# Routed expert layers: joined sums spread over loop turns, row counts placed later, three scatter buffers

## The reference

```python
logits = einsum('bsh,he->bse', x, rw) + rb
vals, idx = top_k(softmax(logits), 2);  vals = vals / vals.sum(-1)
xhat = (x - mean(x)) * rsqrt(var(x) + EPS)
xe = xhat[None] * g + b                                   # per expert
h = gelu(einsum('ebsh,ehf->ebsf', xe, w1) + b1)
y = einsum('ebsf,efh->ebsh', h, w2) + b2
x = einsum('bsh,ebsh->bsh', comb, x[None] + y)            # comb: the two weights, else 0
```

## Time and profile before

| | us |
|---|---|
| median of 3 runs (1640.12 to 1645.81) | 1641.62 |
| the profiled execution | 1646.7 |
| its span | 1644.9 |
| TensorE busy, share of the span | 1418.8, 86% |
| VectorE busy | 1274.0, 77% |
| ScalarE busy | 1120.4, 68% |
| POOL busy | 847.8, 52% |
| mean granted TensorE clock | 0.932 |

### The profile page before, as it was taken

How to read it: one execution, slowest core, us unless ns; L and a number is a source line. 1 busy time by engine, 2 the same in 40 slices (tenths; PEclk the granted TensorE clock), 3 DMA queues, 4 the chain that set the end, 5 groups by cost and what they waited for, 6 DMA issues and landing times.

```text
span 1644.9 us, 36942 instructions
## 1 busy us (share of the span) xinstructions
PE 1418.8 (86%) x11037; PEld 1110.8 (68%) x11037; DVE 1274.0 (77%) x3803; ACT 1120.4 (68%) x1975; POOL 847.8 (52%) x1534
## 2 busy tenths in 40 slices
PE   6999989997779989887999888899989888888882
PEld 4666566667658877666787666678777666766661
DVE  6987888894478887878887877887887888676773
ACT  4443443440858988666898866688988668999871
POOL 2256566765745564234556513355652337787345
PEclk9998998995889999989999998999999899999986
DMA  7963666612858766545786754478766446876532
GB/s 285 397 228 129 260 236 236 269 31 56 222 154 247 229 223 185 179 134 175 208 262 204 216 184 135 131 232 258 233 209 190 141 140 189 206 206 170 168 64 20
DMA packets 181110, 314.11 MB, mean 191 GB/s; under 512 B 37569, under 2 KB 117809, under 8 KB 180529
## 3 DMA queue, kind: packets, MB, share of 16 engines
q1 hardware_dynamic: 159408, 288.27, 55.2%
q0 software_dynamic: 21504, 23.48, 6.2%
HBM read 205.20 MB, written 113.72 MB: 194 GB/s over the span
## 4 chain that ended last, share of the span: by engine, by line
PE 38%; DVE 14%; issue 13%; ACT 7%; POOL 3%; POOLq 0%; ACTq 0%; DVEq 0%
PE ps_h L1817 5%; PE ps_h L1819 5%; PE ps_h L1818 5%; PE ps_q L1850 5%; PE ps_y L1831 5%; PE ps_y L1833 5%; PE ps_y L1832 5%; ACT xh L1373 3%; DVE row L1505 3%; ACT hh L1395 2%; DVE hl L1468 2%; PE ps_t L1804 1%; DVE pbn L1474 1%; DVE row L1533 1%; PE ps_q L1848 1%
## 5 line engine op out<-in xcount | busy, mean ns | idle before, releaser
L1389 ACT ACTIVATE hg<-ps_h,bb 128x512 f32<-128x512 f32 x592 | 389.1, 684 | 225.4 <-PE ps_h L1819 224.4
L1468 DVE TENSOR_TENSOR hl<-hg,hh 128x1024 fp32r<-128x1024 f32 x296 | 360.6, 1220 | 200.2 <-ACT hh L1395 200.0
L1395 ACT ACTIVATE hh<-hg 128x1024 fp32r<-128x1024 f32 x296 | 313.1, 1058 | 3.3 <-PE ps_y L1833 0.9
L1303 POOL DMA_INDIRECT regions<-nrow,posi x192 | 228.9, 1192 | 85.3 <-issue 48.0
L1817 PE MATMUL ps_h<-xTh,w1b 128*128 128x512 f32 x592 | 261.9, 442 | 8.4 <-ACT hg L1389 7.0
L1819 PE MATMUL ps_h<-xTh,w1b 128*128 128x512 f32 x592 | 239.2, 404 | 0.0
L1818 PE MATMUL ps_h<-xTl,w1b 128*128 128x512 f32 x592 | 238.9, 403 | 0.0
L1831 PE MATMUL ps_y<-hh,w2b 128*128 128x512 f32 x592 | 238.8, 403 | 0.0
L1832 PE MATMUL ps_y<-hl,w2b 128*128 128x512 f32 x592 | 236.7, 400 | 0.0
L1833 PE MATMUL ps_y<-hh,w2b 128*128 128x512 f32 x592 | 236.7, 400 | 0.0
L1850 PE MATMUL ps_q<-ir,yb 128*128 128x140 f32 (+2 forms) x888 | 145.6, 298 | 102.0 <-DVE base L1576 61.9
(11 more groups left out here) (277 smaller groups left out, 2652.2 us busy)
## 6 DMA issues: line engine op xcount, KB each, us to landing
w1b<-w_split SPq DMA_DIRECT2D x148, 512.0 KB, 3.7
w2b<-w_split SPq DMA_DIRECT2D x148, 512.0 KB, 4.4
regions<-zero SPq DMA_DIRECT2D x14, 4326.0 KB, 24.6
row<-regions SPq DMA_DIRECT2D x84, 294.0 KB, 4.3
w_split<-wst SPq DMA_DIRECT2D x32, 512.0 KB, 5.1
wr<-in_L_ffn_w_dram SPq DMA_DIRECT2D x32, 256.0 KB, 4.9
regions<-regions SPq DMA_DIRECT2D x24, 294.0 KB
x<-in_L_attn_x_dram SPq DMA_DIRECT2D x16, 256.0 KB, 3.7
```

The source lines that it names most:

```text
L1303: g.indirect_dma_start(out=regions[layer % 2], out_offset=bass.IndirectOffsetOnAxis(ap=posi[r % 2][:, b:b + 1], axis=0), in_=nrow[r % 2][: ...
L1389: a.activation(hg[c // 2 % PAIRS][:, c % 2 * TILE:(c % 2 + 1) * TILE], ps_h[c % BANKS][:], ACT.Gelu, bias=bb[h % BBUFS][:, c % FC:c % FC + ...
L1395: a.activation(hh[j % PAIRS][:], hg[j % PAIRS][:], ACT.Identity).then_inc(hi, 1)
L1468: v.tensor_tensor(hl[n][:], hg[n][:], hh[n][:].bitcast(F32), ALU.subtract).then_inc(lo, 1)
```

## The change

It does six things.

- `joined_sums` becomes `joined_sum(n, q)`, one buffer at a time. Tile 11 + p adds only q = 0 to p (15 of 25 per layer), at pairs given by `SUM_AT`, one or two in a pair, at the end of VectorE's pair. `shares_by_class` moves to the end of the pair before the first update.
- The count of a main tile that two main tiles follow moves from its end + 10 to + 14 chunks (behind the third round of the next tile), and its `place` and `rows_out` from + 8 to + 11 pairs. Tiles 9, 10 and 15 stay where they were. `oh` gets two buffers.
- `nrow` and `posi`, and the semaphores of the scatter, become three.
- The table's pieces move: `early_counts` by one pair, `early_tiles` by two; the late pieces stand in every other pair, from pair 9 of a layer (10 in the first) to 17 (18).
- The second layer's biases are folded in attention tiles 7 to 10, POOL adds them at tile 12 (`second_biases`); `later_biases(1)` goes; SP waits for one more signal before it stores them.
- The last `make_u` stands ahead of VectorE's addition of the remaining biases.

```diff
+SUMS = [(p, q) for p in range(NX) for q in range(p + 1)]
+SUM_AT = [57, 59, 61, 63, 65, 65, 67, 69, 69, 71, 73, 73, 75, 77, 77]
+OUTS = 3
...
-                return t - 3 if 3 <= t < 3 + E else None
+                return t - 3 if 3 <= t < 3 + 2 * E else None
...
+                make_u(NT - 1, 3 * NT - 1)
                 dve.wait_ge(s_b1late_ps, 1)
-                v.tensor_tensor(bst[:, E:, 0:FC], ps_b1[:, 0:(L - 1) * K].rearrange("p (n c) -> p n c", c=FC),
-                                cols[:, K:L * K].rearrange("p (n c) -> p n c", c=FC), ALU.add).then_inc(s_bias, 1)
-                make_u(NT - 1, 3 * NT - 1)
+                v.tensor_tensor(bst[:, 2 * E:, 0:FC], ps_b1[:, 0:(L - 2) * K].rearrange("p (n c) -> p n c", c=FC),
+                                cols[:, 2 * K:L * K].rearrange("p (n c) -> p n c", c=FC), ALU.add).then_inc(s_bias, 1)
...
                 rows_T(NT)
-                later_biases(1)
                 project(NT - 1)
...
-            nrow = [esb(f"nrow{q}", [P, NB, W]) for q in range(2)]
+            nrow = [esb(f"nrow{q}", [P, NB, W]) for q in range(OUTS)]
...
+            def count_at(m):
+
+                return START[m + 1] + (14 if main(m + 1) and main(m + 2) and PLACE[m] < NT - 1 else 10)
+
+            def place_at(m):
+
+                return START[m + 1] // 2 + (11 if main(m + 1) and main(m + 2) and PLACE[m] < NT - 1 else 8)
+
+            COUNTED = {count_at(n): n for n in range(N) if routed(n)}
+            PLACED = {place_at(n): n for n in range(N) if routed(n)}
+
             def counted_before(c):
 
-                return NT + len([n for n in range(N) if routed(n) and START[n + 1] + 10 < c])
+                return NT + len([at for at in COUNTED if at < c])
...
                     if routed(m):
                         gates(tile_of(m) + NT)
-                        rows_out(tile_of(m) + NT, layer(m) + 1)
                     if last_layer(m):
                         add_to_output(m)
+                    m = PLACED.get(j)
+                    if m is not None:
+                        rows_out(tile_of(m) + NT, layer(m) + 1)
...
-                def joined_sums(n):
+                def joined_sum(n, q):
 
                     p, cols_ = PLACE[n] - FULL, width(n)
-                    dve.wait_ge(p_xh, n + 1)
-                    dve.wait_ge(upd, ROUND0[n])
+                    if q == 0:
+                        dve.wait_ge(p_xh, n + 1)
+                    dve.wait_ge(upd, ROUND0[layer(n) * NU + FULL + q + 1])
+                    link(dve)
                     r = row[n % ROWBUFS]
-                    for q in range(NX):
-                        chained(v.scalar_tensor_tensor(r[:, :, 0:cols_], joined[q][:, :, 0:cols_], belongs[:, q, p:p + 1], r[:, :, 0:cols_], ALU.mult, ALU.add))
+                    chained(v.scalar_tensor_tensor(r[:, :, 0:cols_], joined[q][:, :, 0:cols_], belongs[:, q, p:p + 1], r[:, :, 0:cols_], ALU.mult, ALU.add))
...
                     if main(n) and part == 1:
-                        dve.wait_ge(s_scat[m % 2], (m + NT) // 2 * NB * 16 if routed(n) else (L * NT) // 2 * NB * 16)
+                        q = (m + NT) % OUTS
+                        dve.wait_ge(s_scat[q], min((m + NT) // OUTS, len(range(q, L * NT, OUTS))) * NB * 16)
...
-                    m = ENDS.get(2 * (j - 8))
-                    if routed(m):
+                    m = PLACED.get(j)
+                    if m is not None:
                         place(tile_of(m) + NT)
...
                     for l in range(L):
-                        late = j - START[l * NU] // 2 - (8 if l else 10)
+                        late = j - START[l * NU] // 2 - (9 if l else 10)
                         if late == 0:
                             wait(dve, t_base, (l + 1) * NT)
                             late_counts()
                             late_tiles(l)
-                        if late == 1:
+                        if late == 2:
                             joins_of_tiles(l)
-                        if late == 2:
+                        if late == 4:
                             row_parts()
-                        if late == 3:
+                        if late == 6:
                             row_values(0)
-                        if late == 4:
+                        if late == 8:
                             row_values(1)
                             row_experts(l)
...
+                    for l in range(L):
+                        for (tile, q), at in zip(SUMS, SUM_AT):
+                            if at == j - START[l * NU] // 2:
+                                joined_sum(l * NU + FULL + NX + tile, q)
+                    n = ENDS.get(2 * (j - 3))
+                    if main(n) and gathered(n):
+                        shares_by_class(n)
+                    n = ENDS.get(2 * (j - 4))
+                    if joins_in(n if n is not None else -1):
+                        shares_by_class(n)
...
-                    m = ENDS.get(c - 10)
-                    if routed(m):
-                        count(tile_of(m) + NT, oh)
+                    m = COUNTED.get(c)
+                    if m is not None:
+                        count(tile_of(m) + NT, oh[tile_of(m) % 2])
```

More of the change, by code:

```diff
@@ L101, in sandwich_kernel @@
         a_nd, a_th, a_posf = (sb(n, [P, NB]) for n in ("a_nd", "a_th", "a_posf"))
-        a_posi = [sb(f"a_posi{q}", [P, NB], I32) for q in range(2)]
+        a_posi = [sb(f"a_posi{q}", [P, NB], I32) for q in range(OUTS)]
         num, full, used, cum, cumx, cumr = (sb(n, [P, NC]) for n in ("num", "full", "used", "cum", "cumx", "cumr"))
@@ L138, in sandwich_kernel @@
         t_cnt, t_pos, t_row, t_base, t_tab = (sem(f"t_{n}") for n in ("counts_psum", "position", "row", "base", "table"))
-        s_scat = [sem(f"rows_out{q}") for q in range(2)]
+        s_scat = [sem(f"rows_out{q}") for q in range(OUTS)]
         s_c0, s_c1, s_consts = sem("constants_blank"), sem("constants_numbers"), sem("routing_constants")
@@ L289, in a_place @@
             pool.wait_ge(t_pos, m + 1)
-            wait(pool, s_scat[m % 2], m // 2 * NB * 16)
-            nc.gpsimd.tensor_scalar(a_posi[m % 2][:], a_posf[:], BIG, None, ALU.add).then_inc(t_row, 1)
+            wait(pool, s_scat[m % OUTS], m // OUTS * NB * 16)
+            nc.gpsimd.tensor_scalar(a_posi[m % OUTS][:], a_posf[:], BIG, None, ALU.add).then_inc(t_row, 1)
         def a_rows_out(pool, m, some):
@@ L816, in transposes @@
                     wait(pe, z_cnt, t - 3)
-                    wait(pe, s_b1x, min(max(t - 3, 0), E))
+                    wait(pe, s_b1x, min(max(t - 3, 0), 2 * E))
                     for b in range(NB):
@@ L859, in logits_and_counts @@
                         pe.wait_ge(s_w1, 16)
+                        if e >= E:
+                            pe.wait_ge(s_w1all, (L - 1) * 16)
+                        weights, at = (w1s, e * F) if e < E else (w1all, (e - E) * F)
                         for c in range(FC):
-                            last = mm(ps_a[:, FOLD.start + c:FOLD.start + c + 1], w1s[:, e * F + c * P:e * F + (c + 1) * P],
+                            last = mm(ps_a[:, FOLD.start + c:FOLD.start + c + 1], weights[:, at + c * P:at + (c + 1) * P],
                                       cols[:, LNB + e:LNB + e + 1], start=True, stop=True)
@@ L1047, in sandwich_kernel @@
             dd, cc, mm2, pd, tq, tr = (esb(n, [P, NB, CL]) for n in ("dd", "cc", "mm2", "pd", "tq", "tr"))
-            oh = esb("oh", [P, NB + 1, CL], BF16)
+            oh = [esb(f"oh{q}", [P, NB + 1, CL], BF16) for q in range(2)]
             ndiff, th, posf = (esb(n, [P, NB]) for n in ("ndiff", "th", "posf"))
-            posi = [esb(f"posi{q}", [P, NB], I32) for q in range(2)]
+            posi = [esb(f"posi{q}", [P, NB], I32) for q in range(OUTS)]
             late_rows, part_len, part_cum, part_at, off = (esb(n, [P, NS]) for n in ("late_rows", "part_len", "part_cum", "part_at", "off"))
@@ L1136, in scattered @@
             def scattered(eng, r):
-                for q in range(2):
-                    done = (r - q) // 2 + 1
+                for q in range(OUTS):
+                    done = (r - q) // OUTS + 1
                     wait(eng, s_scat[q], done * NB * 16)
@@ L1277, in prior_rows_out @@
                 def prior_rows_out(r):
-                    wait(pool, s_scat[r % 2], r // 2 * NB * 16)
+                    wait(pool, s_scat[r % OUTS], r // OUTS * NB * 16)
                 def identify(m):
@@ L1318, in _ @@
                 a_place(pool, NT - 3)
-                g.memset(oh[:, NB, :], 0.0)
                 for q in range(2):
+                    g.memset(oh[q][:, NB, :], 0.0)
+                for q in range(OUTS):
                     g.memset(nrow[q][:, :, width(0):LW], 0.0)
```

67 lines of the change are left out of this document (34 added, 33 removed).

## The result

Faster: 1606.9 us (median of 4, 1604.93 to 1607.18) against 1643.7 (median of 4); the ratio is 0.977, interval 0.975 to 0.980. The forecast was 1597, the range 1562 to 1628. The profiled execution took 1607.03 where the one of before took 1646.7, so 39.7 us went, where the sum said 44.8.

The account below looks back on a forecast made before the run. TensorE bounds the expert part, its largest named wait being output rounds waiting for `base` (61.9 us). Terms 53.1 - 15.3 - 4 + 9 + 2 = 44.8; 1646.7 - 44.8 - 5.1 = 1596.8, so 1597 us, range 1562 to 1628.

Parts of the forecast that it names:

- term 1: Main tiles: `place` moved behind VectorE's fourth pair's rest makes TensorE's first round wait 1.36, tiles cost about 14.9: -15.3 us.
- term 2: Five tiles with joined sums: 15 spread sums instead of 25 per layer, 76.7 us against 95.4 and 93.4: +53.1 us.
- third rival: The clock falls: new waits of 1.36 lower TensorE's clock on 39 tiles, costing 90 us: 1687, slower; chance 0.06.
- Term 3: Two tiles with tables: late counts move a pair, join numbers fall ahead of the next first update: -4 us.
- Term 4: Third scatter buffer: removes tile 10's wait for scattered rows, but `base` is late next there: 0.
- Term 5: Layer 3: spread sums take four waits, some 13 us, from TensorE, but POOL's output scatters set the end: +9 us.
- Term 6: Second layer's biases leave the end of attention for tiles 7 to 10: +6 and -4, so +2 us.
- 1570: Rival: VectorE is further ahead in its fourth pair, so first rounds don't wait: 1570 us; chance 0.20.
- DVE is not the bound: Rival judged: VectorE is the bound, so the five joined tiles gain only half, 26.5: 1623 us; chance 0.16.
- The clock rival: Same as the third rival: short waits drop TensorE to the lower clock level: 1687 us; chance 0.06.
- The sums do not block: Rival judged: a sum waits for a join's update or normalized rows, tiles stay at 19: about 1640 us; chance 0.03.

Follow-up runs that it names:

- Run 2: The kernel after with `place` ahead of the weights' rest instead of behind it, in the same VectorE pair: 1573.6 us, ratio 0.960.
- run 1: The kernel after with the count and `place` back where they were before, sums still spread and three buffers kept: 1571.9 us, ratio 0.959.
- run 5: As run 1, with the fifteen sums moved to VectorE's second pair of a tile and the light pairs before the first joined tile: 1557.0 us, ratio 0.943.
- run 6: As run 5, with the later table pieces four pairs apart, each in VectorE's second pair, row moves one weight half later: 1538.9 us, ratio 0.934.
- Run 8: As run 1, with two buffers for rows to scatter instead of three: 1579.9 us, ratio 0.960.
- runs 7: Second layer's biases back at the end of attention, in the kernel after (1602.7 us) and in that of run 6 (1537.3 us; 1539.7 beside it).

## Why the prediction was right, and where not

The verdict held, the mechanism of term 1 held in the quiet tiles, and that of term 2 in the main. That the sum came out only 5.1 too high is partly luck: term 1 was 14.0 too hopeful, and the rest together 8.9 too cautious. Term by term, forecast and measured:

**Term 1, `place` in turn D: -15.3, measured -29.3.** In the quiet tiles the start of the first round was forecast to the hundredth. DVE's turn C, D and `place`, then PE's first round:

```profile
531.41 1.23 DVE L1491 TENSOR_TENSOR hl<-hg,hh 128x1024 fp32r<-128x1024 f32 x1 [1.80 <-ACT hh L1418]
...
535.98 1.22 DVE L1491 TENSOR_TENSOR hl<-hg,hh 128x1024 fp32r<-128x1024 f32 x1
537.11 0.22 DVE L1595 TENSOR_TENSOR tq<-ps_q,base 128x64 f32<-128x64 f32 x1
```

```profile
537.82 0.36 PE L1883 MATMUL ps_q<-ir,yb 128*128 128x140 f32 x1 [0.94 <-DVE base L1598]
```

From turn C the round starts at 537.82 - 531.41 = 6.41, as forecast; the wait itself is 0.94, not 1.36, and the tile takes 14.76 to 14.8 against 14.9. What failed is the step "one more wait falls on the first join half": it priced J0 like a quiet tile, at 1.3. J0's window took 10.4 instead of 6.9, for two reasons in its rows.

```profile
591.05 1.23 DVE L1491 TENSOR_TENSOR hl<-hg,hh 128x1024 fp32r<-128x1024 f32 x1 [1.66 <-ACT hh L1418]
592.95 0.69 DVE L1507 TENSOR_TENSOR xTl<-ps_t,xTh 128x512 fp32r<-128x512 f32 x1 [0.68 <-ACT xTh L1403]
...
596.99 1.22 DVE L1491 TENSOR_TENSOR hl<-hg,hh 128x1024 fp32r<-128x1024 f32 x1
598.12 0.22 DVE L1595 TENSOR_TENSOR tq<-ps_q,base 128x64 f32<-128x64 f32 x1
```

```profile
598.83 1.47 PE L1883 MATMUL ps_q<-ir,yb 128*128 128x140 f32 x6 [1.87 <-DVE base L1598]
...
600.52 0.63 PE L1851 MATMUL ps_h<-xTl,w1b 128*128 128x512 f32 x1
```

First, join halves are short, so the next one's low part (`xTl`, with a wait of 0.68 for ScalarE) falls into turn C, ahead of `choose`; `place` starts 7.07 after turn C instead of 5.70, and PE waits 1.87. Second, behind that wait the matmul takes 0.63: the 1.2 GHz level, for some 3 us. This is the third rival's mechanism, in one place of a layer. Run 2 takes one rest out of the way: wait 0.74, clock up, 22.0. The forecast also left out the first round of tile 10, which falls into J2's window and waits 0.7 there: 7.8 instead of 6.9. The second slip is tile 5: its window went from 14.3 to 18.5, 17.5 and 17.4, since the last table pieces now stand one or two turns ahead of `place` (waits of 3.05, 2.04 and 2.04, each with the 1.2 GHz level behind it), which the forecast had put under the tables. In run 1, with `place` back, the same pieces still make it 16.4, 15.3 and 14.5, so a part of this slip is the tables' own. Beyond the forecast, J0 to J2 lost 8.5 and tile 5 lost 8.7; the other tiles lost 3.2 less than priced.

**Term 2, the sums apart: +53.1, measured +57.3.** The five tiles took 13.4, 15.2, 15.7, 15.7 and 15.7 where 13.8, 15.2 and three of 15.9 were forecast. The granted clock was 1.00, as forecast, though the row that this went by was misread (see the rivals). The reason given for the last three, `place` in turn D on top of the sums, was only half of it: with `place` back in turn A (run 1) they still take 15.5, because then `base` is late for the second round. What holds them is the sums in turn D: run 5 moves only these (the shares stay) and gets 13.9. So the 15.9 came out close with half of its reason wrong.

**Term 3, tables: -4, measured -3.2.** Run 1 shows that the wider spacing itself brought nothing (35.1, 34.1 and 31.9 against 34.9, 34.5 and 32.2 before): `joins_of_tiles` in turn D put a wait in the place of the old one. In the kernel after it is 4.16, with the 1.2 GHz level behind it. In turn B `joins_of_tiles` is free (run 6).

```profile
768.28 1.70 PE L1883 MATMUL ps_q<-ir,yb 128*128 128x136 f32 x6 [4.16 <-issue]
```

**Term 4, the third buffer: 0; not measured by itself.** The reason given fits the trace: in the kernel after DVE waits for no scattered rows, and tile 10's window (15.4 instead of 15.9 in the first layer) has a wait of 1.06 for `base`. Run 8 puts 6 us on the buffer with `place` in turn A.

**Term 5, layer 3: +9, measured +13.7**: 10.8 at the end, and 2.9 before it that the forecast did not have.

**Term 6, biases: +2; a profile against a profile gave -2.2**, but that lies within what attention varies by itself. The pair of runs 7 could not tell it from zero either.

A further 3.4 (the windows of tiles 0 to 3 of layer 0, and J3 to tile 12) was not forecast. Added up, 44.8 - 14.0 + 4.2 + 0.8 + 4.7 - 4.2 + 3.4 = 39.7. The other 5 us between 1597 and 1607 are the step from the profiled execution to the median: it stood 5.1 above the median of the three runs before the change (3.0 above that of the four in the result), and at the median after it.

**The rivals.** First rounds do wait (0.94), so 1570 fell, though run 2 comes near it by one step's place. DVE is not the bound (run 5). The clock rival fell in the quiet tiles: behind waits of 0.94 the granted clock stayed at 1.00. It came true at J0 and tile 5. The prediction held it off with one row, 0.40 after a wait of 2.97, and wrote that the fall came only after the longer waits. That reading was wrong: the trace of before already had the 1.2 GHz level behind a wait of 1.86, in tile 10's window of layer 1.

```profile
883.26 1.05 PE L1850 MATMUL ps_q<-ir,yb 128*128 128x136 f32 x4 [1.86 <-issue]
...
884.54 0.63 PE L1818 MATMUL ps_h<-xTl,w1b 128*128 128x512 f32 x1
```

The rule of the Trainium skill named with the rival (TensorE: Matmul & The Clock Gate, "A second HAM failure mode: psum-queue depth-cycling"), that frequent short idles let the clock swing, finds no support in the quiet tiles, which wait 0.94 once in 14.8 us and do not swing. Nor do the tiles with sums, three of which wait twice each (0.95 and 0.66 in tile 15) at a granted clock of 1.00; more frequent waits no run here shows. The sums do not block: the longest idle time of DVE ahead of one is 0.1.

## What to carry to other kernels

On an engine that works through a written order, what an added instruction costs depends on what stands behind it in its turn, more than on its length: with the same sums a tile took 15.5 or 13.9 us by the turn they stood in. Before a wait is moved, look at what the engine that releases it has ahead of it in every kind of turn, the odd ones at the joints of the loop above all; and time a change of several parts with each part taken back, since here one part gave back about half of what another gained.

## What the runs showed of the hardware that was not expected

The length of a wait alone does not tell whether TensorE's clock falls. In the kernel after, the round at 627.03 waited as long as J0's (1.88) and the matmul behind it was still at 0.39, the 2.4 GHz level; in the kernel before, it was 0.39 after 3.45 (at 765.61) and 0.63 after 1.86 (at 883.26, above). No wait under 1.8 before an output round of the kernel after was followed by the 1.2 GHz level.

```profile
627.03 0.72 PE L1883 MATMUL ps_q<-ir,yb 128*128 128x140 f32 x4 [1.88 <-ACT yb L1424]
627.82 0.39 PE L1851 MATMUL ps_h<-xTl,w1b 128*128 128x512 f32 x1
```

Attention, whose code is the same in nine of these profiles (after, and all runs but the two with the biases back), ended between 411.8 and 424.9, and the granted clock went with it: between 100 and 200 us it was 0.90 to 0.95 in the five that ended by 418.2, and 0.84 to 0.86 in the four that ended later. Which of the two brings about the other, no run shows. The expert part repeats far better: 1118.5 and 1118.3 in two profiles of the same kernel, whose spans were 6.1 apart. A change of a few us is read there, not from the span.
